# Decays inside the mixer's blocks: four matmuls per block, or a broadcast fetch and three elementwise engines

## What is computed

```python
dt = clip(softplus(dt + dt_bias), 0, 100);  Adt = -exp(A_log) * dt        # per token and head
A_cum = cumsum(Adt within a chunk of 64)
L = exp(segsum(Adt))              # L[l, s] = exp(A_cum[l] - A_cum[s]) for l >= s, else 0
M = (C @ B.T) * L                 # per head
Y_diag = M @ (x * dt)
Y_off = (C @ carried states) * exp(A_cum)
y = Y_diag + Y_off + D * x
```

## Time and profile before

| | us |
|---|---|
| three runs, median (lowest, highest) | 1626.34 (1622.86, 1626.49) |
| profiled execution, its own time | 1625.54 |
| its span on the core | 1623.7 |
| TensorE clock granted, mean | 0.998 of full |
| PE, DVE, ACT, POOL busy, share of the span | 98%, 66%, 41%, 27% |

### The profile page before, as it was taken

How to read it: one execution, slowest core, us unless ns; L and a number is a source line. 1 busy time by engine, 2 the same in 40 slices (tenths; PEclk the granted TensorE clock), 3 DMA queues, 4 the chain that set the end, 5 groups by cost and what they waited for, 6 DMA issues and landing times.

```text
span 1623.7 us, 25033 instructions
## 1 busy us (share of the span) xinstructions
PE 1596.7 (98%) x9580; PEld 1297.7 (80%) x9580; DVE 1077.3 (66%) x2050; ACT 665.0 (41%) x992; POOL 442.2 (27%) x330
## 2 busy tenths in 40 slices
PE   7999999999999999999999999999999999999999
PEld 4788888877888778888877888877888878778887
DVE  7543445676676876778777677777676686866543
ACT  5334443473333464334365333346343351343321
POOL 1666652011221212222112121221221222354300
PEclk9999999999999999999999999999999999999999
DMA  7855654755455455555545555545555546542434
GB/s 278 319 198 201 233 195 170 271 188 164 163 167 171 146 173 165 171 167 163 175 126 188 178 159 164 177 151 193 160 178 164 171 138 190 160 137 86 128 104 156
DMA packets 236647, 283.68 MB, mean 175 GB/s; under 512 B 15472, under 2 KB 191728, under 8 KB 227952
## 3 DMA queue, kind: packets, MB, share of 16 engines
q1 hardware_dynamic: 236528, 282.07, 52.3%
HBM read 231.18 MB, written 50.86 MB: 174 GB/s over the span
## 4 chain that ended last, share of the span: by engine, by line
PE 67%; DVE 8%; ACT 2%; issue 1%; DMA 1%; SPq 1%; ACTq 0%; DVEq 0%
PE bank L1290 22%; PE bank L1246 11%; PE bank L1336 11%; PE bank L1373 6%; PE bank L1471 5%; PE bank L1350 3%; PE bank L1534 2%; PE bank L1489 2%; PE bank L1511 2%; PE bank L1527 1%; DVE m_cv L2172 1%; DMA cum_stay<-m_aS 1%; DVE m_sta L2216 1%; DVE m_sta L2218 1%; PE bank L1499 1%
## 5 line engine op out<-in xcount | busy, mean ns | idle before, releaser
L1290 PE MATMUL bank<-fxT,wj 128*128 128x512 f32 x1608 | 384.1, 392 | 0.0
L1290 PEld LDWEIGHTS bank<-fxT,wj 128*128 128x128 f32 x1608 | 299.3, 188 | 63.9
L1246 PE MATMUL bank<-xT,wi 128*128 128x512 f32 x900 | 225.4, 399 | 4.5 <-DVE m_cv L2172 4.2
L1336 PE MATMUL bank<-m_wd,m_hb 128*128 128x512 f32 x864 | 216.5, 393 | 1.0 <-DVE m_hb L2073 0.8
L1246 PEld LDWEIGHTS bank<-xT,wi 128*128 128x128 f32 x900 | 168.3, 190 | 43.0 <-issue 8.0
L1770 ACT CAST m_hb<-xn 128x512 fp32r<-128x512 f32 x76 | 47.0, 620 | 353.2 <-DVE xn L2067 345.6
L1336 PEld LDWEIGHTS bank<-m_wd,m_hb 128*128 128x128 f32 x864 | 160.4, 188 | 34.8 <-issue 2.1
L2543 POOL TENSOR_TENSOR m_L<-m_L,m_GT 128x512 f32<-128x512 f32 x36 | 52.8, 1466 | 439.1 <-ACT m_L L1820 439.1
L2080 DVE TENSOR_TENSOR res<-bank,res 128x512 f32<-128x512 f32 x148 | 101.9, 689 | 31.3 <-PE bank L1336 29.3
L1820 ACT ACTIVATE m_L<-bank 128x512 f32<-128x512 f32 x128 | 76.5, 598 | 85.7 <-PE bank L1489 85.1
L1764 ACT ACTIVATE xn<-bank,sc 128x512 f32<-128x512 f32 x76 | 52.3, 688 | 122.1 <-PE bank L1290 116.5
(11 more groups left out here) (278 smaller groups left out, 2690.3 us busy)
## 6 DMA issues: line engine op xcount, KB each, us to landing
wj<-ug_split SPq DMA_DIRECT2D x155, 512.0 KB, 4.3
m_wd<-dn_split SPq DMA_DIRECT2D x43, 1024.0 KB, 4.9
wi<-in_split SPq DMA_DIRECT2D x76, 512.0 KB, 3.3
ug_split<-b_wu SPq DMA_DIRECT2D x8, 2048.0 KB, 13.4
m_wo<-out_split SPq DMA_DIRECT2D x32, 512.0 KB, 4.1
in_split<-b_msp SPq DMA_DIRECT2D x20, 512.0 KB, 3.7
wi<-ug_split SPq DMA_DIRECT2D x17, 512.0 KB, 4.1
raw<-in_wug SPq DMA_DIRECT2D x8, 1024.0 KB, 6.9
```

The lines of the kernel that those rows point to most:

```text
L1246: ins = pe.matmul(to[:], w[:, a, k, :], xT[:, b, k, :], start=(k == 0 and i == 0), stop=(k == KH - 1 and i == 2))
L1290: ins = pe.matmul(to[:], w[:, a, k, :], frm[:, b, k, :], start=(k == 0 and i == 0), stop=(k == KH - 1 and i == 2))
L1336: ins = pe.matmul(down_bank(at, t)[:], hb[:, a, j, ck(t)], w[:, b, j, :], start=(j == 0 and n == 0), stop=(j == 1 and n == 2))
```

## The change

The matmuls `decay`, their operands `mvg` and `stn` and the small DMAs `heads` go. The running sums are scaled by A once on ACT (`scaled_sums`), in place, and written to memory once. For each block `later_sums` fetches the running sums of 8 heads into `L` itself, each row copied to 64 partitions: two DMAs of 512 KB. PE turns the running sums once for a sequence (`turn_sums`, four transposes) and DVE keeps them as columns in `cst` (`keep_first`, four small copies). Then, for the pairs of heads j = 0 to 3:

- `since`: L - cst, with cst repeated along 64 tokens; j = 0, 1 on DVE as its last work of the block before, j = 2, 3 on POOL ahead of its `add_squares` and `combine`;
- `decay_after` on ACT: relu(-L), four instructions, ahead of
- `decay_exp` on ACT: exp(-L), four instructions as before but from SBUF;
- `times_g`: all four on DVE; the mask of later tokens is now put into `GT` when it is kept.

`sums_low` and some set-up at the mixer's start go. Cut to its core:

```diff
             def keep(q):
-                sp.wait_ge(s_cu, q + 1)
+                sp.wait_ge(s_ah, q + 1)
                 wait(sp, s_eb, 16 * NB * q)
-                sp.dma_start(cum_d, du[0:HEADS, :]).then_inc(s_kp, 16)
-                sp.wait_ge(s_as, q + 1)
-                for l in range(2):
...
+                wait(sp, s_ld, 32 * NB * q)
+                sp.dma_start(cum_d, aS).then_inc(s_kp, 16)
...
-            def heads(q, b):
...
+            def later_sums(q, b):
+                wait(sp, s_Y, NB * q + b - 1)
+                wait(sp, s_su, 2 * (NB * q + b))
+                wait(sp, s_sg, 2 * (NB * q + b))
+                src = cum_d[HPB * b:HPB * (b + 1), :].rearrange("(j e) s -> e j s", e=2)
+                for e in range(2):
+                    sp.dma_start(L[half(e), b % 2, :, :], src[e].unsqueeze(0).to_broadcast([HALF, QUADS, SEQ])).then_inc(s_ld, 16)
...
-            def decay(q, b, j):
...
-                pe.matmul(A[:], stn[:, j, :], mvg[:], start=True, stop=True).then_inc(s_A, 1)
...
+            def turn_sums(q):
+                pe.wait_ge(s_ah, q + 1)
...
+                for c in range(NPC):
+                    ins = pe.transpose(S[1][:, HEADS * c:HEADS * (c + 1)], aS[:, ck(c)], cs[HEADS:P, C_I4 + HEADS:C_I4 + P])
+                ins.then_inc(s_tc, 1)
...
+            def decay_after(q, b, j):
+                act.wait_ge(s_su if j < 2 else s_sg, 2 * (NB * q + b) + j % 2 + 1)
+                act.activation(L[:, b % 2, j, :], L[:, b % 2, j, :], ACT.Relu, scale=-1.0).then_inc(s_L, 1)
             def decay_exp(q, b, j):
...
-                act.activation(L[:, b % 2, j, :], A[:], ACT.Exp).then_inc(s_L, 1)
+                act.wait_ge(s_L, 2 * QUADS * (NB * q + b) + j + 1)
+                act.activation(L[:, b % 2, j, :], L[:, b % 2, j, :], ACT.Exp, scale=-1.0).then_inc(s_L, 1)
...
+            def since(q, b):                                   # DVE
+                dve.wait_ge(s_ld, 32 * (NB * q + b + 1))
+                if b == 0:
+                    dve.wait_ge(s_cst, q + 1)
+                for j in range(2):
+                    to = L[:, b % 2, j, :].rearrange("p (k l) -> p k l", k=NK)
+                    frm = cst[:, :, QUADS * b + j:QUADS * b + j + 1].to_broadcast([P, NK, QL])
+                    dve.tensor_tensor(to, to, frm, ALU.subtract).then_inc(s_su, 1)
+            def keep_first(q):
+                dve.wait_ge(s_tc, q + 1)
...
+                for e in range(2):
+                    for i in range(2):
+                        ins = dve.tensor_copy(cst[half(e), i:NK:2, :],
...
-                dve.tensor_copy(GT[:], X[:]).then_inc(s_gt, 1)
+                dve.tensor_tensor(GT[:].rearrange("p (k l) -> p k l", k=NK), X[:].rearrange("p (k l) -> p k l", k=NK),
+                                  msk[:].unsqueeze(1).to_broadcast([P, NK, QL]), ALU.mult).then_inc(s_gt, 1)
...
+                    times_g(q, b, 3)
...
+                    if not end:
+                        since(q, b + 1)                        # DVE, last of block b
...
                     if older:
                         low_part(*older)
+                    if b < NB - 1:
+                        since(q, b + 1)                        # POOL
+                    if older:
                         add_squares(*older)
                     combine(q, b)
```

More of the change, by code:

```diff
@@ L863, in _, with mixer @@
             add(n, (2, 3))
-def mixer(nc, s, ug_s, dn_s, wsc, in_s, out_s, cum_m, cum_d, cum_s, out):
-    res, cs, pr, banks, ones, acol, aex, xn, xT, fxT, win, wj, sc = (
-        s[n] for n in "res cs pr banks ones acol aex xn xT fxT wi wj sc".split())
+def mixer(nc, s, ug_s, dn_s, wsc, in_s, out_s, cum_d, out):
+    res, cs, pr, banks, ones, acol, xn, xT, fxT, win, wj, sc = (
+        s[n] for n in "res cs pr banks ones acol xn xT fxT wi wj sc".split())
     s_g, s_wi, s_wj, s_in = s["gate"], s["wi_full"], s["wj_full"], s["projected"]
@@ L919, in mixer @@
         L = sb("L", [P, 2, 4, SEQ])
-        dw, dl, de, dtf = (L[:, 0, i, :] for i in range(4))
-        mvg, stn = sb("mvg", [P, SEQ], F32R), sb("stn", [P, QUADS, P], F32R)
+        dw, dl = (L[:, 0, i, :] for i in range(2))
+        de, dtf = sb("de", [P, SEQ])[:], sb("dtf", [P, SEQ])[:]
+        cst, msk = sb("cst", [P, NK, PAIRS]), sb("msk", [P, QL])
         xd, sta = sb("xd", [P, NPC, P]), sb("sta", [P, NS, P])
@@ L1172, in _ @@
                     if not end:
-                        heads(q, b + 1)
+                        later_sums(q, b + 1)
                     if b < NB - 2 or more:
@@ L1190, in _ @@
                     keep(q + 1)
-                    heads(q + 1, 0)
+                    later_sums(q + 1, 0)
                     carried_sums(q + 1, 0)
@@ L1582, in _ @@
             products(0)
+            turn_sums(0)
             turn_d(0)
-            pe.wait_ge(s_c0, 3)
-            pe.wait_ge(s_z0, 4)
             for q in range(BATCH):
@@ L1614, in _ @@
                         down(at - 1, 1)
-                        decay(q, b, 1)
                         down(at - 1, 2)
@@ L1618, in _ @@
                             turn_tile(q + 1, 1)
-                        decay(q, b, 2)
                         down(at - 1, 3)
@@ L1622, in _ @@
                             turn_tile(q + 1, 2)
-                        decay(q, b, 3)
                         if b == 1 and q:
@@ L1673, in _ @@
                 in_proj(q + 1, 4)
+                turn_sums(q + 1)
                 turn_d(q + 1)
@@ L1730, in b_silu @@
                 wait(act, s_mv, NB * q)
-                wait(act, s_mp, NB * q)
                 conv_silu(q, 0, Bf[:])
@@ L1915, in _ @@
             silu(0, 1)
-            sums_high(0)
+            scaled_sums(0)
             raw(0, 2, 0)
@@ L1934, in _ @@
                     older = (q, b - 1) if b else (q - 1, NB - 1) if q else None
+                    for j in range(QUADS):
+                        decay_after(q, b, j)
                     for j in range(QUADS):
@@ L2328, in _ @@
             keep_products(0)
+            keep_first(0)
             keep_rows(0)
-            dve.wait_ge(s_c0, 4)
+            since(0, 0)
+            dve.wait_ge(s_c0, 1)
             for q in range(BATCH):
@@ L2354, in _ @@
                         add_down(at - 1, 2)
-                    if not end:
-                        times_g(q, b, 1)
+                    times_g(q, b, 1)
                     if at == 0:
@@ L2425, in _ @@
                 keep_products(q + 1)
+                keep_first(q + 1)
                 keep_rows(q + 1)
+                since(q + 1, 0)
             other = stats(beside(ITEMS - 1), 1)
```

139 lines of the change are left out of this document (41 added, 98 removed).

## The result

The changed kernel took 1682.19 us (median of four runs, 1678.73 to 1687.63) against 1626.41: a ratio of 1.0352 (95% interval 1.0337 to 1.0368), 56 us slower. The forecast was 1671. One run of the kernel before took 4137.27 us; it counts in this median of four, not in the ratio. The profiled execution was the slowest of the four, 1687.63 us with a span of 1685.9; that span is 62.2 us above the one of before, so that the profiled executions lie some 6 us further apart than the medians.

A forecast was written before the change was run, and what follows sets the result against it. VectorE's spare time, not just TensorE's 98% busy time, was taken to decide. Terms -7.7 + 27.3 + 10.4 + 10.5 + 1 + 4 = +45.5 us on 1625.54 gave 1671 us; range 1630 to 1700.

The forecast's parts named there:

- The path: TensorE idles ahead of `down` 2 for `add_down` 0; block 0's `scaled_end` delays `new_states`; blocks 2, 4, 6 gain 7.7 us.
- Blocks 1, 3 and 5: With block 2 of the first sequence, 13 blocks: `scaled` comes late and TensorE idles, +2.1 us each, +27.3 us.
- I take 4.9: Blocks 1, 3, 5: the 1 MB fetch lands 4.9 us after issue, within bounds of 3.3 and 9.0.
- The list: Block 5: VectorE and GpSimd alternate instructions; fetch landing after 3.3 us gives +0.2, 4.9 gives +2.1, 9.0 gives +0.9.
- The clock: Block 0: idle TensorE brings the lower clock, 3 x 1.3 = +4 us.
- a rival of 22 us more: Clock falls in blocks 1, 3, 5 and 7 too: 17 x 1.3 = 22 us more, 1693 us; chance 0.20.
- Block 7: Relus and late `since` ahead of exp 0 and `turn_tile` 0: next `in_proj` +2.6 us each, +10.4 us.
- Block 0: `keep_first` and `since` delay `scaled_end`; next `in_proj` 3.5 us later: 3 x 3.5 = +10.5 us, first sequence +1.
- The early fetch isn't what ends last here: Block 0: one write in place of five lets the fetch go 4 us sooner than `heads`.
- with blocks 0 and 7 unchanged: Faster rival, new work hidden behind TensorE: 1608 us if blocks 0 and 7 stay unchanged, 1597 with all; chance 0.12.
- The other rivals: Light collisions, early fetch: 1634 us, chance 0.24; no collisions: 1622 us, 0.08; faster, new work hidden: 1597 us, 0.12.
- The case of a table load for relu: ScalarE, each block: 1.28 us more if relu needs its own table, some 25 us on top; chance 2 in 100.

The follow-up runs named there:

- e3_quarter_fetch: Changed kernel with only a quarter of the fetch, 256 KB a block in place of 1 MB, from the third block on: 1669.0 us, ratio 1.0258.
- e6_no_relu: Changed kernel with the fetch issued ahead of two weight loads and without ScalarE's four relus a block: 1647.9 us, ratio 1.0129 against the kernel before.
- e12_keep_earlier: Changed kernel with fetch a block earlier, block 0 reordered, relus and since ahead for block 7, running sums written ahead of a weight load: 1662.5 us, ratio 1.0235.

## Why the prediction was right or wrong

- **The path** was right where TensorE is kept waiting: `down` waits for `add_down` 0, `new_states` for `scaled_end`, and the blocks behind an `out_proj` gain (-7.5 against -7.7).
- **Blocks 1, 3 and 5** came out near the forecast (+30.6 against +27.3), and that is luck. The step that failed is "I take 4.9" for the fetch. The two DMAs take 7.7 us in the median, the second of a pair 9.2 and up to 11.1, so the fetch lands up to 2.1 us behind `hidden_low`, and what ends last is the landing, not `combine`. The list had that case as "after 9.0 us both engines start together and it is +0.9". Without the clock's 13 us the group is at +17, 1.3 a block where 2.1 was forecast; the clock, forecast at nothing here, adds 1.0 a block. Two errors of opposite sign met. The collisions that were forecast are real (`e3_quarter_fetch`, 1.1 us a block without the clock at a landing of 4.1 us, where the list gives 0.2 for 3.3 us and 2.1 for 4.9), but in the changed kernel the landing hides them.
- **The clock** was +4 in the sum, and a rival of 22 us more at 0.20. 24.3 us against 3.4 before is +21: 7.6 more in blocks 0, where 4 was forecast, and 13.3 in 8 of the 13 middle blocks, 1.4 to 1.7 each in place of 1.3, none in block 7. So the rival was more than half true. The price had been read from six matmuls of the one place where the clock falls in the kernel before, while all of that place lost 3.4 us. The argument against the rival, that the only fall followed two stretches with little between, didn't hold.
- **Block 7** was right in mechanism (`e6_no_relu`), and over-priced by 0.7 us a block: `turn_tile` 0 moved by 2.1 us, not 3.1.
- **Block 0** is half of the cost and was forecast at half its size: without the clock some 24 us against 11.5. The step that failed is "The early fetch isn't what ends last here: one write in place of five lets it go 4 us sooner than `heads`". The fetch went 1.0 to 2.6 us sooner in sequences two to four, and its landing, 7.0 to 7.4 us for the second DMA in place of `m_stn`'s 1.8, came last: VectorE waited 2.5 to 5.3 us for it. `e3_quarter_fetch` gives 10 of the 32 us back with a quarter of the fetch in three of the four. The rest was not taken apart piece by piece; `e12_keep_earlier` shows that even with everything in the best order that I found, `times_g` end 3.1 to 3.5 us after `ydiag` is wanted (7.8 in the first sequence), and that the clock then costs 4.4 to 4.7 more.
- **The sum** came within 11 us (1671 against 1682): block 0 is short by 16, the middle blocks 3, block 7 is 3 too high, and the profiled execution, from which these are read, lies 5 above the median. The range (1630 to 1700) held. One number among the rivals doesn't follow: with blocks 0 and 7 unchanged, 24 blocks of 0.88 give 1604, not 1608.
- **The other rivals** are out: the fetch landed neither early nor without company, and VectorE's `since` took 1.1 us each beside GpSimd's, 0.6 alone. The case of a table load for relu is out as well.

## What to carry to other kernels

When a fetch of 64 KB becomes one of 1 MB, price its landing from loads that share its place and company in the queue, by the last of its DMAs, and ask at once what waits for it; a moved buffer isn't late until the engine in front of it is the one with 1 us to spare. Two delays that each end at the same wait hide each other: taking one away can show the other in place of a gain. In these traces VectorE and GpSimd took turns where both read two operands from SBUF: work shared between them was added, and a collision that was moved away came back where GpSimd ran next. An idle stretch of TensorE of 1.8 to 3.5 us could cost again in the lower clock behind it: 1.4 to 1.7 us in 8 of 13 middle blocks of the changed kernel, 4.4 to 4.7 in the blocks 0 of `e12_keep_earlier`.

## What the runs showed of the hardware

- `since`, with one operand repeated along 64 tokens, costs VectorE the same 0.61 to 0.63 us as any other of 128x512 with two SBUF operands (four in 2.50).
- A DMA of 512 KB landed in 7.7 us from broadcast rows in runs of 2 KB and in 7.6 from distinct rows in runs of 4 KB: copying the same rows to 64 partitions didn't lengthen the landing.
- The clock did not fall behind each idle stretch of the same length: in the changed kernel it fell in block 2 of the first sequence (2.98 us idle) and not in block 5 (3.02), and it fell behind stretches of 1.84 us in blocks 3 and 5 of the fourth. Eight falls in thirteen blocks can be priced as a share; from these traces they can't be forecast block by block.
